# A GRU in front of a transformer block: the n gate's input products gather in bank 4, and ScalarE copies them over

## The chip, the cores and the metric

One core of one Trainium2 chip runs the whole program. The metric is the device time of one execution in microseconds. The kernel before takes 801.4 us, the median of 3 runs (801.28 to 802.28).

## The reference, cut to what matters

16 sequences of 128 time steps with 256 features each go through a GRU, and the result, added to its input, through one transformer block (layer norm with modulation, 16 heads of attention, an MLP). The change is in the GRU, which is a chain over 128 time steps:

```python
def cell(h, x):
    gi = x @ W_ih + b_ih            # 256 -> 768, needs only the input
    gh = h @ W_hh + b_hh            # 256 -> 768, needs the state
    i_r, i_z, i_n = split(gi, 3); h_r, h_z, h_n = split(gh, 3)
    r = sigmoid(i_r + h_r)
    z = sigmoid(i_z + h_z)
    n = tanh(i_n + r * h_n)
    return (1 - z) * n + z * h
```

The n gate is the one in which the input product and the state product can't be added before the gate r is known.

## The kernel before, in words

The 128 time steps are cut into 16 blocks (`r` in the code, `NBL`) of 8 steps (`s`, `BS`). The state lies turned: 128 partitions, and 32 columns `j` (two halves of the features, 16 sequences each). All products are made of float16 halves: `high*high`, `low*high` and `high*low`.

Each block has three PSUM banks, and they alternate between two sets, so that the next block's input products can be made while this block runs. The r bank and the z bank hold 8 x 32 columns each, and in them 16 columns of an output tile lie together. The n bank holds 8 x 32 pairs: in each pair, element 0 takes the state's product and element 1 the input's. VectorE's scan at L986 reads the pairs in order, with r beside them, and so forms `r*h_n + i_n` in one instruction. Because of the pairs, an input product of the n gate (`gate_cols`, `m` 4 or 5) writes every second column of its bank.

What one step does, and on which engine (a "step" below runs from one `h_hi` scan to the next):

- TensorE: `gru_step` issues 36 matmuls of 16 columns (24 at L439 with `h_hi`, 12 at L446 with `h_lo`), and waits for the state `h_hi` first. Behind them come the steps' other products: the transposes of a finished block at step 0 (L393) and at step 5, the bias of the next block's banks at step 1 (`x_bias`, L373), and from step 2 on the next block's input products (`x_products`, L386): 36 a block, of 128 columns each. `share` says how many: 9, 9, 7, 1, 5, 5 at the steps 2 to 7. The order `products` goes through the output tiles `m` = 0 to 5, so the n gate's 12 (tiles 4 and 5) come last: one at step 4, one at step 5, five at each of the steps 6 and 7.
- ScalarE: the sigmoid of r (L761), of z and of minus z (L763, L764), the tanh (L766), and then one piece of work beside the chain: the high half of the next x, of a stretch of weights, or of a finished block's rows (L731, a 128x256 copy out of PSUM). At step 3 there is none.
- VectorE: the scan `npre` (L986, behind a wait at L984), `nu` (L992), the scan `h_hi` (L998), the same in float32 (L1000), `h_lo` (L1003), and then work beside the chain.

The order on each engine is written out by hand, and semaphores tie the engines. In the last block TensorE has no input products; at its steps 1 to 4 it makes the modulation's products (`modulation`, L414) in bank 4. The attention and the MLP follow, on the same banks.

Of the kernel before, what the change touches and what calls it, by code (L numbers as in the profile page):

```python
# [15 lines left out]
P = 128  # L16
B, T, D = 16, 128, 256
KD = D // P
GATES = 3 * D
GM = GATES // P  # L20
# [8 lines left out]
BS = 8  # L29
NBL = T // BS  # L30
GB = KD * B
# [7 lines left out]
GK = 32 + 2 * GM  # L39
# [22 lines left out]
def build(nc, x, cols_in, gate_rows, W_ih, W_hh, ada_a, ada_r, ada_b, weights, out):  # L62
# [3 lines left out]
    with ctx:  # L66
# [29 lines left out]
        gpair = sb("gpair", [GK, P], f16, gru)  # L96
        sel = sb("sel", [GK, 2 * GM], f32, gru)
        selrz = sb("selrz", [GK, 4], f32, gru)
        pick = sb("pick", [GK, 4 * GB], f16, gru)
# [79 lines left out]
        def sems(names):  # L179
            return [sem(n) for n in names.split()]  # L180
# [11 lines left out]
        (r_mm, hn_mm, z_mm, r_ok, z_ok, n_ok, npre_ok, u_ok, hhi_ok, h32_ok, hlo_ok) = sems(  # L192
            "r_mm hn_mm z_mm r_ok z_ok n_ok npre_ok u_ok hhi_ok h32_ok hlo_ok")

        xt_hi, xt_lo = sems("xt_hi xt_lo")

        xr_ok, lb_T, lb_st, lb_ag, lb_ve, lb_r, lb_a, lb_b, lb_B, lb_hi, lb_lo = sems(
            "xr_ok lb_T lb_st lb_ag lb_ve lb_r lb_a lb_b lb_B lb_hi lb_lo")
# [15 lines left out]
        r_cols, z_cols = ([ps[:, 0:BS * GB].rearrange("p (t j) -> p t j", t=BS) for ps in pair]  # L214
                          for pair in (r_bank, z_bank))
        n_cols = [ps[:, :].rearrange("p (t j s) -> p t j s", t=BS, s=2) for ps in n_bank]
        row_ps, back_ps = bank[5][:, 0:D], bank[5][:, D:2 * D].rearrange("p (k c) -> p k c", k=KD)

        xr_v = xr[:, :, :, :].rearrange("p k n (b t) -> p k b n t", b=B)
# [142 lines left out]
        def _(pe):  # L362
            def product(ps, w, a, start, stop):
# [3 lines left out]
                mm(ps, w[1], a[0], start=False, stop=False, skip_group_check=True)  # L367
                return mm(ps, w[0], a[1], start=False, stop=stop, skip_group_check=True)  # L368

            def x_bias(n):  # L370

                for ps, at, width in ((r_bank, 0, GB), (z_bank, GB, GB), (n_bank, 2 * GB, 2 * GB)):
                    nc.tensor.matmul(ps[n % 2][:, 0:BS * width], gpair[:, :],  # L373
                                     pick[:, at:at + width].unsqueeze(1).broadcast_to([GK, BS, width]), start=True,
                                     stop=False, skip_group_check=True)

            def gate_cols(n, m):

                c = slice(m % 2 * B, (m % 2 + 1) * B)
                return (r_cols[n % 2][:, :, c], z_cols[n % 2][:, :, c], n_cols[n % 2][:, :, c, 1])[m // 2]  # L380

            def x_products(n, order):

                for m, k, i in order:
                    w, a = ((wih_hi, xb_hi), (wih_lo, xb_hi), (wih_hi, xb_lo))[i]
                    nc.tensor.matmul(gate_cols(n, m), w[:, k, m * P:(m + 1) * P], a[:, n % 2, k, :], start=False,  # L386
                                     stop=False, skip_group_check=True)

            def rows_T(n):

# [19 lines left out]
            def modulation(tiles):  # L410

                for m in tiles:
                    for k in range(KD):
                        mm = nc.tensor.matmul(bank[4][:, m * B:(m + 1) * B], adar[:, k, (m - G1) * P:(m - G1 + 1) * P],  # L414
                                              condT[:, k, :], start=(k == 0), stop=(k == KD - 1))
                if tiles[-1] == ADA - 1:
                    mm.then_inc(ada_mm, 1)
# [44 lines left out]
                high(2, slice(2, 8))  # L462
                low(2).then_inc(z_mm, 1)

            products = [(m, k, i) for m in range(GM) for k in range(KD) for i in range(3)]
            share = (0, 0, 0, 9, 18, 25, 26, 31, 36)
            for r in range(NBL):
                for s in range(BS):
                    gru_step(r, s)
                    if s == 0 and r > 0:  # L470
                        if r == 1:
                            pe.wait_ge(rows_ok, 2)
                        rows_T(r - 1)
                    elif s == 5 and r > 0:
                        rows_back(r - 1)
                    if r < NBL - 1:
                        if s == 1:
                            x_bias(r + 1)
                        elif s == 2:
                            pe.wait_ge(xt_lo, r + 2)  # L480
                        x_products(r + 1, products[share[s]:share[s + 1]])
                    if r == 0 and s == 3:
                        pe.wait_ge(adaw_in, 32)
                        pe.wait_ge(small_in, 16)
                        row_modulation(0)
                    elif r == 0 and s == 5:
                        row_modulation(1)
                    elif r == NBL - 1 and s in (1, 2, 3, 4):
                        if s == 1:
                            pe.wait_ge(rest_in, 16)  # L490
                        modulation(range(2 * s + 2, 2 * s + 4))
            rows_T(NBL - 1)

# [225 lines left out]
        def _(act):  # L719
# [5 lines left out]
            def x_high(n):  # L725
                act.wait_ge(x_in[n % 4], (n // 4 + 1) * 16)
                nc.scalar.activation(xb_hi[:, n % 2, :, :], x32[:, n % 4, :, :], copy).then_inc(xt_hi, 1)

            def y_high(n):
                act.wait_ge(lb_B, n + 1)  # L730
                nc.scalar.activation(y_hi[:, :, :, n * BS:(n + 1) * BS],  # L731
                                     back_ps.rearrange("p k (b t) -> p k b t", b=B), copy).then_inc(lb_hi, 1)
# [24 lines left out]
            for r in range(NBL):  # L757
                for s in range(BS):
                    t1 = r * BS + (s + 1)
                    act.wait_ge(r_mm, t1)  # L760
                    nc.scalar.activation(zr[:, :, 1], r_cols[r % 2][:, s, :], ACT.Sigmoid).then_inc(r_ok, 1)  # L761
                    act.wait_ge(z_mm, t1)
                    nc.scalar.activation(zg[:, :], z_cols[r % 2][:, s, :], ACT.Sigmoid).then_inc(z_ok, 1)  # L763
                    nc.scalar.activation(zz[:, :, 1], z_cols[r % 2][:, s, :], ACT.Sigmoid, scale=-1.0)  # L764
                    act.wait_ge(npre_ok, t1)
                    nc.scalar.activation(nu[:, :, 0], npre[:, :, 1], ACT.Tanh).then_inc(n_ok, 1)  # L766
                    if r == 0 and s == 0:
                        x_high(1)
                    if s == 1 and r < NBL - 2:
                        x_high(r + 2)  # L770
                    elif s in (2, 4, 6, 7):
                        piece_high(r * PB + (2, 4, 6, 7).index(s))
                    elif s == 5 and r > 0:
                        y_high(r - 1)
# [110 lines left out]
        def _(dve):  # L885
# [94 lines left out]
            for r in range(NBL):  # L980
                for s in range(BS):
                    t1 = r * BS + (s + 1)
                    dve.wait_ge(r_ok, t1)
                    dve.wait_ge(hn_mm, t1)  # L984

                    nc.vector.tensor_tensor_scan(npre[:, :, :].rearrange("p j s -> p (j s)"),  # L986
                                                 zr[:, :, :].rearrange("p j s -> p (j s)"),
                                                 n_bank[r % 2][:, s * 2 * GB:(s + 1) * 2 * GB], 0.0,
                                                 ALU.mult, ALU.add).then_inc(npre_ok, 1)
                    dve.wait_ge(z_ok, t1)  # L990
                    before = hs[:, 1 - r % 2, BS - 1, :, 1] if s == 0 else hs[:, r % 2, s - 1, :, 1]
                    tt(nu[:, :, 1], zg[:, :], before, ALU.mult).then_inc(u_ok, 1)  # L992
                    dve.wait_ge(u_ok, t1)
                    dve.wait_ge(n_ok, t1)

                    gates = (zz[:, :, :].rearrange("p j s -> p (j s)"), nu[:, :, :].rearrange("p j s -> p (j s)"),
                             0.0, ALU.mult, ALU.add)
                    nc.vector.tensor_tensor_scan(h_hi[:, :, :].rearrange("p j s -> p (j s)"), *gates  # L998
                                                 ).then_inc(hhi_ok, 1)
                    nc.vector.tensor_tensor_scan(hs[:, r % 2, s, :, :].rearrange("p j s -> p (j s)"), *gates  # L1000
                                                 ).then_inc(h32_ok, 1)
                    dve.wait_ge(h32_ok, t1)
                    tt(h_lo[:, :], hs[:, r % 2, s, :, 1], h_hi[:, :, 1], ALU.subtract).then_inc(hlo_ok, 1)  # L1003
                    if r > 0 and s in row_work:
                        row_work[s](r - 1)
                    if r == 0 and s == 0:
                        x_low(1)
                    if s == 2 and r < NBL - 2:
                        x_low(r + 2)
                    elif s == 6:  # L1010
                        rows_sum(r, slice(0, 6))
                    elif s == 7:
                        rows_sum(r, slice(6, BS))
                    if r == 0 and s in (3, 5):
                        row_modulation(s // 4)
                    elif r == NBL - 1 and s == 5:
                        modulation_sums()
                    elif r == NBL - 1 and s == 7:
                        modulation_gates()
# [214 lines left out]
```

## Time and profile before

| | |
|---|---|
| median of 3 runs | 801.4 us |
| the profiled execution's own time | 801.32 us |
| its span | 799.4 us |
| TensorE busy | 753.2 us (94%) |
| VectorE busy | 580.4 us (73%) |
| ScalarE busy | 470.9 us (59%) |
| GpSimd busy | 101.2 us (13%) |
| granted TensorE clock over the span, as a share of 2.4 GHz | 0.899 |

The GRU takes the first 273 us of the span. "Busy" of TensorE counts matmuls from the start to the modelled end of each, and they overlap, so it says little about idle room; the starts of two matmuls in a row say more. In a row of the timeline the first number is the start and the second the duration, both in us from the span's start. In a row that groups instructions, "| busy, mean ns | idle before, who ended it" stands at the end.

### The profile page before, as it was taken

What the parts mean: (1) busy time and instruction counts of PE and PEld (TensorE: products, weight loads), DVE (VectorE), ACT (ScalarE), POOL (GpSimd) and SP (SyncE); (2) the same over time, 40 slices, a digit from 0 to 9 for tenths busy, and PEclk for the clock granted to TensorE, in tenths of its full rate; (3) what the DMA queues carried; (4) which work ended last, traced back from release to release, by engine and by line L of the source; (5) the groups of instructions that cost most, each with busy time, mean ns of one, the idle gap of its engine ahead of it and who ended that gap; (6) DMA issues with size and microseconds to landing.
All of it is one profiled execution on the core that took longest, in us unless ns stands there. A gap on an engine that the chain in (4) does not pass through costs nothing.

```text
span 799.4 us, 24458 instructions
## 1 busy us (share of the span) xinstructions
PE 753.2 (94%) x10068; PEld 532.7 (67%) x10068; DVE 580.4 (73%) x1548; ACT 470.9 (59%) x1564; POOL 101.2 (13%) x121
## 2 busy tenths in 40 slices
PE   6888989889888889999999999999999999999998
PEld 5777777777777656666666666666667666644445
DVE  5677777777777567777788887788877888853543
ACT  4344444444443266667777667777677776766454
POOL 0221222222222200000030010020010300100130
PEclk9977665766877599999999999999999999999999
DMA  6121121112111012222222222222222222210001
GB/s 221 43 96 42 43 81 43 43 42 78 45 35 37 2 27 41 40 42 41 41 41 40 41 41 41 41 41 41 41 41 41 41 41 41 41 27 26 1 27 53
DMA packets 76566, 36.65 MB, mean 46 GB/s; under 512 B 70395, under 2 KB 73127, under 8 KB 76327
## 3 DMA queue, kind: packets, MB, share of 16 engines
q1 hardware_dynamic: 75879, 33.52, 18.3%
q8 instruction: 79, 1.29, 0.7%
q10 hardware_dynamic: 576, 1.57, 0.6%
q14 instruction: 32, 0.26, 0.1%
HBM read 16.20 MB, written 2.10 MB: 23 GB/s over the span
## 4 chain that ended last, share of the span: by engine, by line
PE 83%; ACT 6%; DVE 5%; DMA 2%; issue 2%; SPq 1%; DVEq 0%; ACTq 0%
PE bank L366 19%; PE bank L367 19%; PE bank L368 19%; PE bank L439 12%; PE bank L386 7%; PE bank L446 5%; DVE h_hi L998 3%; DMA pT_lo<-p_lo 2%; ACT zg L763 2%; ACT prob L812 1%; ACT nu L766 1%; PE bank L373 1%; PE bank L414 1%; ACT zz L764 1%; SPq L257 1%
## 5 line engine op out<-in xcount | busy, mean ns | idle before, releaser
L439 PE MATMUL bank<-h_hi,whh_hi 128*128 128x16 f16 x1536 | 112.8, 177 | 29.0 <-DVE h_hi L998 28.5
L439 PEld LDWEIGHTS bank<-h_hi,whh_hi 128*128 128x128 f16 x1536 | 92.7, 101 | 65.6 <-DVE h_hi L998 65.6
L366 PE MATMUL bank<-y_hi,w_hi 128*128 128x512 f16 (+2 forms) x324 | 122.6, 379 | 1.3 <-ACT hf L845 1.3
L367 PE MATMUL bank<-y_hi,w_lo 128*128 128x512 f16 (+2 forms) x324 | 122.6, 379 | 0.0
L368 PE MATMUL bank<-y_lo,w_hi 128*128 128x512 f16 (+2 forms) x324 | 122.3, 379 | 0.0
L439 PE MATMUL bank<-h_hi,whh_lo 128*128 128x16 f16 x1536 | 110.6, 176 | 0.0
L761 ACT ACTIVATE zr<-bank 128x32 f32<-128x32 f32 x128 | 25.7, 201 | 130.1 <-PE bank L446 130.1
L812 ACT ACTIVATE prob<-bank,nmx 128x128 f32<-128x128 f32 x256 | 90.4, 365 | 19.9 <-DVE nmx L1074 19.9
L439 PEld LDWEIGHTS bank<-h_hi,whh_lo 128*128 128x128 f16 x1536 | 93.4, 101 | 0.1
L366 PE MATMUL bank<-w_hi,y_hi 128*128 128x128 f16 x512 | 89.1, 219 | 0.0
L367 PE MATMUL bank<-w_hi,y_lo 128*128 128x128 f16 x512 | 89.1, 219 | 0.0
L368 PE MATMUL bank<-w_lo,y_hi 128*128 128x128 f16 x512 | 89.0, 219 | 0.0
L820 ACT ACTIVATE qT_hi<-bank,small 128x512 f16<-128x512 f32 x64 | 44.0, 687 | 74.0 <-PE bank L368 74.0
L446 PE MATMUL bank<-h_lo,whh_hi 128*128 128x16 f16 x1536 | 78.6, 176 | 0.0
L296 POOL TENSOR_TENSOR w_lo<-stage,w_hi 128x320 f16<-128x320 f32 x64 | 50.7, 792 | 193.7 <-DVE h_lo L1003 191.5
L986 DVE TENSOR_TENSOR_SCAN npre<-zr,bank 128x64 f32<-128x64 f32 x128 | 36.8, 287 | 47.4 <-ACT zr L761 47.3
L1071 DVE TENSOR_REDUCE mx<-bank 128x4 f32<-128x512 f32 x64 | 44.2, 690 | 29.4 <-PE bank L368 29.4
L386 PE MATMUL bank<-xb_hi,wih_hi 128*128 128x128 f16 x192 | 61.7, 326 | 3.2 <-DVE xb_lo L917 3.2
L386 PE MATMUL bank<-xb_lo,wih_hi 128*128 128x128 f16 x192 | 63.5, 334 | 0.0
L386 PE MATMUL bank<-xb_hi,wih_lo 128*128 128x128 f16 x192 | 62.1, 326 | 0.0
L446 PEld LDWEIGHTS bank<-h_lo,whh_hi 128*128 128x128 f16 x1536 | 59.1, 101 | 0.1
L368 PEld LDWEIGHTS bank<-y_lo,w_hi 128*128 128x128 f16 x324 | 31.8, 98 | 38.3 <-issue 1.0
(142 smaller groups left out, 2092.4 us busy)
## 6 DMA issues: line engine op xcount, KB each, us to landing
stage<-in_weights SPq DMA_DIRECT2D x16, 640.0 KB, 4.1
x<-in_x SPq DMA_DIRECT2D x16, 128.0 KB, 4.3
out<-yT SPq DMA_DIRECT2D x3, 512.0 KB, 2.6
adar<-in_ada_r SPq DMA_DIRECT2D x1, 1024.0 KB, 7.2
pT_hi<-p_hi SPq DMA_TRANSPOSE x64, 2.4
pT_lo<-p_lo SPq DMA_TRANSPOSE x64, 2.4
wih<-in_W_ih ACTq DMA_DIRECT2D x2, 384.0 KB, 4.0
whh<-in_W_hh ACTq DMA_DIRECT2D x2, 384.0 KB, 6.1
```

The lines of the kernel that those rows point to most:

```text
L296: gtt(w_lo[:, j * PC:(j + 1) * PC], stage[:, r % 2, i * PC:(i + 1) * PC], w_hi[:, j * PC:(j + 1) * PC], sub).then_inc(piece_lo, 1)
L366: mm(ps, w[0], a[0], start=start, stop=False, skip_group_check=True)
L367: mm(ps, w[1], a[0], start=False, stop=False, skip_group_check=True)
L368: return mm(ps, w[0], a[1], start=False, stop=stop, skip_group_check=True)
L386: nc.tensor.matmul(gate_cols(n, m), w[:, k, m * P:(m + 1) * P], a[:, n % 2, k, :], start=False, stop=False, skip_group_check=True)
L439: nc.tensor.matmul(out(m0 + m), half[:, k, w], h_hi[:, k * B:(k + 1) * B, 1], start=False, stop=False, skip_group_check=True)
L446: mm = nc.tensor.matmul(out(m0 + m), whh_hi[:, k, (m0 + m) * P:(m0 + m + 1) * P], h_lo[:, k * B:(k + 1) * B], start=False, stop=k == KD - ...
L761: nc.scalar.activation(zr[:, :, 1], r_cols[r % 2][:, s, :], ACT.Sigmoid).then_inc(r_ok, 1)
L812: op = nc.scalar.activation(prob[:, j, :], bank[3][:, j * T:(j + 1) * T], ACT.Exp, bias=nmx[:, j:j + 1], scale=SCALE, accum_out=den[:, j:j ...
L820: nc.scalar.activation(qT_hi[:, :], bank[0][:, :], ident_f, bias=bT[:, BQ + d % H:BQ + d % H + 1]).then_inc(q_h, 1)
L986: nc.vector.tensor_tensor_scan(npre[:, :, :].rearrange("p j s -> p (j s)"), zr[:, :, :].rearrange("p j s -> p (j s)"), n_bank[r % 2][:, s ...
L1071: nc.vector.reduce_max(mx[:, :], bank[3][:, :].rearrange("p (j s) -> p j s", j=QUAD), AX.X).then_inc(s_mx, 1)
```

## The change

The 12 input products of the n gate are made first of a block's 36, and into columns 256 to 511 of bank 4 (`xs_ps`), which nobody else uses in this part, laid out like the r bank: 16 columns of a tile together. Before the first of them a new matmul puts the n gate's input bias there (`side_bias`, 256 columns; its moving operand takes every second column of `pick`). When the last is done, ScalarE copies the 128x256 values into the elements 1 of the next block's n bank (`side_copy`, at step 3). `x_bias` is as before in what it issues. New semaphores: `xs_mm` (products done, ScalarE waits for it) and `xs_ok` (copied; VectorE waits for it before the first scan of a block, TensorE before the next block's `side_bias` and, in the last block, before each of the four modulation calls). Block 0's own products, made before the loop, stay as they were.

```diff
+        xs_ps = bank[4][:, BS * GB:2 * BS * GB].rearrange("p (t j) -> p t j", t=BS)
...
+            def side_bias(n):
+
+                if n > 1:
+                    pe.wait_ge(xs_ok, n - 1)
+                pick_x = pick[:, 2 * GB:4 * GB].rearrange("p (j s) -> p j s", s=2)[:, :, 1]
+                nc.tensor.matmul(xs_ps, gpair[:, :], pick_x.unsqueeze(1).broadcast_to([GK, BS, GB]), start=True,
+                                 stop=False, skip_group_check=True)
             def gate_cols(n, m):
                 c = slice(m % 2 * B, (m % 2 + 1) * B)
+                if m >= 4 and n > 0:
+                    return xs_ps[:, :, c]
                 return (r_cols[n % 2][:, :, c], z_cols[n % 2][:, :, c], n_cols[n % 2][:, :, c, 1])[m // 2]
             def x_products(n, order):
...
+                    if n > 0 and (m, k, i) == (GM - 1, KD - 1, 2):
+                        mm.then_inc(xs_mm, 1)
-            products = [(m, k, i) for m in range(GM) for k in range(KD) for i in range(3)]
+            products = [(m, k, i) for m in (4, 5, 0, 1, 2, 3) for k in range(KD) for i in range(3)]
...
                         elif s == 2:
                             pe.wait_ge(xt_lo, r + 2)
+                            side_bias(r + 1)
...
                     elif r == NBL - 1 and s in (1, 2, 3, 4):
+                        pe.wait_ge(xs_ok, r)
                         modulation(range(2 * s + 2, 2 * s + 4))
...
+            def side_copy(n):
+                act.wait_ge(xs_mm, n)
+                nc.scalar.activation(n_cols[n % 2][:, :, :, 1], xs_ps, copy).then_inc(xs_ok, 1)
...
+                    elif s == 3 and r < NBL - 1:
+                        side_copy(r + 1)
...
                     dve.wait_ge(r_ok, t1)
                     dve.wait_ge(hn_mm, t1)
+                    if s == 0 and r > 0:
+                        dve.wait_ge(xs_ok, r)
```

## Rows read from the trace of the kernel before

**Rows 1.** The page: the chain that ended last, by line; ScalarE's sigmoid of r.
```profile
PE bank L366 19%; PE bank L367 19%; PE bank L368 19%; PE bank L439 12%; PE bank L386 7%; PE bank L446 5%; DVE h_hi L998 3%; DMA pT_lo<-p_lo 2%; ACT zg L763 2%; ACT prob L812 1%; ACT nu L766 1%; PE bank L373 1%; PE bank L414 1%; ACT zz L764 1%; SPq L257 1%
...
L761 ACT ACTIVATE zr<-bank 128x32 f32<-128x32 f32 x128 | 25.7, 201 | 130.1 <-PE bank L446 130.1
```

**Rows 2.** Stretches: start:end, length, busy of each engine, granted clock, DMA.
```profile
12.11:255.28 243.17, 216.07 (x4972) 179.01 (x4970) 175.46 (x729) 105.12 (x569) 55.20 (x72) 0.71 0.18 54
...
273.35:278.60 5.25, 4.64 (x14) 2.18 (x15) 2.90 (x12) 0.38 (x1) 0.70 (x2) 0.50 0.02 5
```

**Rows 3.** Timeline of VectorE in block 15: the scans that end its steps.
```profile
256.98 0.29 DVE L998 TENSOR_TENSOR_SCAN h_hi<-zz,nu 128x64 f16<-128x64 f32 x1
258.96 0.29 DVE L998 TENSOR_TENSOR_SCAN h_hi<-zz,nu 128x64 f16<-128x64 f32 x1
261.00 0.29 DVE L998 TENSOR_TENSOR_SCAN h_hi<-zz,nu 128x64 f16<-128x64 f32 x1
263.67 0.29 DVE L998 TENSOR_TENSOR_SCAN h_hi<-zz,nu 128x64 f16<-128x64 f32 x1
...
271.03 0.29 DVE L998 TENSOR_TENSOR_SCAN h_hi<-zz,nu 128x64 f16<-128x64 f32 x1
273.06 0.29 DVE L998 TENSOR_TENSOR_SCAN h_hi<-zz,nu 128x64 f16<-128x64 f32 x1
```

**Rows 4.** Timeline where step 2 of block 8 ends, at the low clock.
```profile
148.47 0.29 DVE L998 TENSOR_TENSOR_SCAN h_hi<-zz,nu 128x64 f16<-128x64 f32 x1
148.47 0.31 PE L386 MATMUL bank<-xb_hi,wih_lo 128*128 128x128 f16 x1
...
148.58 0.31 PE L386 MATMUL bank<-xb_lo,wih_hi 128*128 128x128 f16 x1
...
148.82 0.19 PE L439 MATMUL bank<-h_hi,whh_hi 128*128 128x16 f16 x1
```

**Rows 5.** Timeline: n gate products (low clock, 7.7); r and z products (high clock, 13.2).
```profile
142.29 0.50 PE L386 MATMUL bank<-xb_hi,wih_lo 128*128 128x128 f16 x1
142.51 0.50 PE L386 MATMUL bank<-xb_lo,wih_hi 128*128 128x128 f16 x1
...
228.02 0.22 PE L386 MATMUL bank<-xb_lo,wih_hi 128*128 128x128 f16 x1
228.07 0.22 PE L386 MATMUL bank<-xb_hi,wih_hi 128*128 128x128 f16 x1
```

**Rows 6.** By line: duration in ns (min/median/max); moving operand stepped, then packed.
```profile
L439 PE MATMUL bank<-h_hi,whh_hi x1536: 168/174/302, 12.3 to 272.2; 128*128 128x16 f16 x192
...
L446 PE MATMUL bank<-h_lo,whh_hi x1536: 168/174/189, 12.9 to 272.3; 128*128 128x16 f16 x192
```

**Rows 7.** Stretches of steps 6-7, 0-1, 2-3, 4-5; first and last of 14.
```profile
41.34:45.30 3.96, 3.24 (x82) 2.69 (x82) 3.04 (x13) 1.99 (x10) 0.79 (x1) 1.00 0.00 0
...
251.26:255.28 4.02, 3.96 (x82) 3.41 (x82) 3.05 (x14) 1.95 (x10) 0.79 (x1) 0.60 0.01 4
...
29.37:33.34 3.97, 2.93 (x77) 2.27 (x77) 2.79 (x13) 1.58 (x9) 0.79 (x1) 1.00 0.00 0
...
239.07:243.19 4.12, 3.41 (x77) 2.43 (x77) 2.90 (x13) 1.25 (x8) 0.79 (x1) 0.84 0.03 6
...
33.34:37.37 4.03, 3.95 (x90) 3.59 (x90) 2.87 (x14) 1.59 (x9) 1.47 (x2) 0.58 0.43 104
...
243.19:247.25 4.06, 4.06 (x91) 3.68 (x90) 2.54 (x14) 1.59 (x9) 1.34 (x2) 0.50 0.40 102
...
37.37:41.34 3.97, 2.96 (x82) 2.46 (x82) 3.10 (x14) 1.90 (x10) 0.80 (x1) 1.00 0.26 100
...
247.25:251.26 4.01, 3.26 (x84) 2.69 (x82) 3.08 (x14) 1.88 (x10) 0.79 (x1) 0.82 0.17 67
```

**Rows 8.** By line: VectorE's stand-alone wait; ScalarE's copy out of PSUM.
```profile
L984 DVEq EVENT_SEMAPHORE  x128: 21/21/21, 13.3 to 272.3; - x128
...
L731 ACT ACTIVATE y_hi<-bank x15: 364/366/384, 40.9 to 269.0; 128x256 f16<-128x256 f32 x15
```

More of the change, by code:

```diff
@@ L193, in build @@
             "r_mm hn_mm z_mm r_ok z_ok n_ok npre_ok u_ok hhi_ok h32_ok hlo_ok")
-        xt_hi, xt_lo = sems("xt_hi xt_lo")
+        xt_hi, xt_lo, xs_mm, xs_ok = sems("xt_hi xt_lo xs_mm xs_ok")
         xr_ok, lb_T, lb_st, lb_ag, lb_ve, lb_r, lb_a, lb_b, lb_B, lb_hi, lb_lo = sems(
@@ L368, in product, with bias_rows @@
                 return mm(ps, w[0], a[1], start=False, stop=stop, skip_group_check=True)
+            def bias_rows(ps, at, width):
+                nc.tensor.matmul(ps, gpair[:, :], pick[:, at:at + width].unsqueeze(1).broadcast_to([GK, BS, width]),
+                                 start=True, stop=False, skip_group_check=True)
             def x_bias(n):
[L372 to L375, printed above, removed]
+                bias_rows(r_bank[n % 2][:, 0:BS * GB], 0, GB)
+                bias_rows(z_bank[n % 2][:, 0:BS * GB], GB, GB)
+                bias_rows(n_bank[n % 2][:, :], 2 * GB, 2 * GB)
+            def side_bias(n):
[4 more added lines that the diff above has]
+                                 stop=False, skip_group_check=True)
             def gate_cols(n, m):
                 c = slice(m % 2 * B, (m % 2 + 1) * B)
+                if m >= 4 and n > 0:
+                    return xs_ps[:, :, c]
                 return (r_cols[n % 2][:, :, c], z_cols[n % 2][:, :, c], n_cols[n % 2][:, :, c, 1])[m // 2]
@@ L385, in x_products @@
                     w, a = ((wih_hi, xb_hi), (wih_lo, xb_hi), (wih_hi, xb_lo))[i]
-                    nc.tensor.matmul(gate_cols(n, m), w[:, k, m * P:(m + 1) * P], a[:, n % 2, k, :], start=False,
-                                     stop=False, skip_group_check=True)
+                    mm = nc.tensor.matmul(gate_cols(n, m), w[:, k, m * P:(m + 1) * P], a[:, n % 2, k, :], start=False,
+                                          stop=False, skip_group_check=True)
+                    if n > 0 and (m, k, i) == (GM - 1, KD - 1, 2):
+                        mm.then_inc(xs_mm, 1)
             def rows_T(n):
```

## The prediction

> **What bounds the kernel now.** I read the page's chain of waits first. Besides the attention's and the MLP's matmuls it holds the GRU's lines: TensorE at L439 and L446, VectorE's scan at L998, ScalarE at L763 and L766, and TensorE at L386 with 7% [rows 1]. The last is the line that the change speeds up, so the question is whether these products are really on the way. For that I went to the timeline, one step at a time. The change lies wholly in the GRU.
>
> A step is a ring: the state `h_hi`, 36 small matmuls, the sigmoid of r, the scan `npre`, the tanh, the scan `h_hi`. The reader should see in [rows 3] that it takes one of two times. From 256.98 to 258.96 it is 1.98 us, from 271.03 to 273.06 it is 2.03 us. The granted clock makes the difference: 1.98 at 2.4 GHz, 2.03 at 1.2 GHz. Over blocks 0 to 14 the granted clock is 0.71 on average, so about 42% of the 120 steps run at the high level ((0.71 - 0.5) / 0.5) [rows 2].
>
> The input products fill the time in which TensorE waits for the ring. At the end of step 2 of block 8, at the low clock, the last product starts at 148.58. Products of this kind follow each other every 107 ns there (148.47, 148.58, rounded), so TensorE is done taking columns at 148.69. The new state is there at 148.76 (148.47 + 0.29), and the next step's first matmul starts at 148.82 [rows 4]. TensorE has 0.13 us to spare. This is the fullest kind of step. Steps with five slow n gate products hold nothing up either: steps 6 and 7 of block 14 last 4.02 us together, which is one step of 1.98 and one of 2.03 [rows 7]. So the products of L386 are in the chain of waits only as TensorE's previous instruction, not as what sets the step's length. **A faster n gate product is worth nothing by itself.**
>
> **The change part by part.** All sums are against the profiled execution's own time, 801.32 us, which is 0.1 us under the median of 801.4; I use the median as the base.
>
> *The n gate's products become faster.* An n gate product takes 0.22 us to the next at the low clock (142.29 to 142.51, with 0.50 us of duration); an r or z product takes 0.107 [rows 4], and 0.05 at the high clock (228.02 to 228.07) [rows 5]. In the new place 16 columns lie together as in the r bank, so I take the r bank's spacing. Per block 12 x 0.107 = 1.3 us of TensorE's time goes at the low clock, 12 x 0.053 = 0.6 us at the high one. All of it lies beside the ring, in steps 4 to 7: directly 0 us. Bounds: it can't lose, since nothing waits longer, and can't gain, since those steps are already 1.98 or 2.03 long like the bare steps of block 15 [rows 3].
>
> *The new bias matmul.* It has 256 columns and stands in step 2, the fullest one: twice an r product's spacing, 0.21 us, at the low clock. The spare room is 0.13 us, so the next step's 36 matmuls start 0.08 us late, and they head the ring, so all of it passes on. Nearly every step 2 is at the low clock: the stretches of steps 2 and 3 have 0.58 and 0.50 in the first and the last of 14, and 0.53 on average [rows 7]. 15 x 0.08 = **+1.2 us**. At the high clock the nine products take half the time and it would be hidden. Ends: 0, if the clock is high; 15 x (0.08 + 0.21) = +4.4, if the stepped read of `pick` halves its speed. A stepped read of float16 stands in the trace: `h_hi` is read at every second column and `h_lo` packed, and both take 174 ns in the median, where at half the speed 16 columns at 1.2 GHz would cost 13 ns more [rows 6]. So I take the full speed.
>
> The Trainium skill says the same in "SBUF — State Buffer", section "Door 1: The DMA port swizzle": TensorE's operands can step without loss as long as two reads fall into one 16-byte line. And on the other side PSUM's lines are 8 bytes, which it says slows matmuls with any gaps; the 0.22 against 0.107 agrees. By that rule too the bias costs 1.2 and not 4.4.
>
> *ScalarE's copy.* 128x256 out of PSUM took 366 ns at L731 [rows 8]; here it also writes into PSUM with gaps, which no row shows: between 0.37 us and twice that. It comes after the tanh in step 3, where ScalarE has no other work. Its products are done by then: the third product of step 3. ScalarE is idle 130.1 us before 128 sigmoids of r, 1.02 us each [rows 1], and that time, of a step without side work even more, covers both ends. Behind it in the queue is only the next sigmoid. Cost 0; twice the copy would still fit.
>
> *The new waits.* TensorE's (before `side_bias`) and ScalarE's are met long before. VectorE's at step 0 is met too (the copy is at step 3 of the block before), but it makes one more stand-alone wait just before the scan `npre`, which is in the ring. Such a wait is 21 ns [rows 8]; a hand-over by semaphore is 60 ns (148.76 to 148.82) [rows 4]. I take 0.03 x 15 = **+0.45 us**, with ends 0 and 0.9. Four TensorE waits in block 15: under 0.05 together.
>
> *What the change does to the clock.* This is the part that the page hides. In the blocks 1 to 14 I took the granted clock of the stretches of two steps, and averaged the 14: 0.70 in steps 6-7, 0.79 in steps 0-1, 0.53 in steps 2-3, 0.78 in steps 4-5 [rows 7]. The two high stretches each come behind one in which TensorE never rests at the low clock: 3.96 us busy of 4.02 in steps 6-7 and 4.06 of 4.06 in steps 2-3. The two in which it falls come behind stretches with 2.93 of 3.97 and 2.96 of 3.97. So the clock follows TensorE's work with a delay, and steps 6-7 owe their work to the slow writing of ten n gate products, 0.21 us each. With 0.107 they lose half of it and look like the steps 4-5 do now. Then the rise in steps 0-1 goes, and part of the level in steps 6-7. The high share in steps 0-1 is (0.79 - 0.5) / 0.5 = 0.6 of 30 steps, 18; I let 15 of them go, and of 12 in steps 6-7 let 9 go, while steps 2-5 stay as they are. 24 steps x 0.045 us (between 1.98 and 2.03) = **+1.1 us**. Ends: all of the 50 high steps go, +2.3; all 70 low ones become high, -3.2.
>
> *Block 15.* Its modulation products fill TensorE at the low clock. Steps there take 2.67 us (261.00 to 263.67) where a bare one takes 2.03; step 1, whose products ran at the high clock, cost nothing extra (258.96 to 261.00 is 2.04) [rows 3]. That high clock came from the n gate products of block 14's steps 6-7. Without it this step too costs 0.64: **+0.65 us**, with ends 0.65 and -1.9 (three slow steps become free).
>
> Sum: 1.2 + 0.45 + 1.1 + 0.65 = **+3.4 us**, so 801.4 + 3.4 = **804.8 us**. The stretch at the low clock behind the GRU (5.25 us [rows 2]) can come out up to 1 us longer or shorter, as the end of the GRU meets the rise of the clock.
>
> The Trainium skill ("TensorE: Matmul & The Clock Gate", section "What's actually happening") says that the clock is low by default, that work releases it and that idleness takes it back. That the work must stay away for it to fall would be another result: TensorE has no long idle stretch in either kernel, so the clock part would be 0. The trace speaks against that, as it falls behind stretches that are 74% busy.
>
> **The rivals.**
>
> *The clock stays as it is.* For it: why the clock falls is read from 14 stretches of one execution, and total work changes by little over a tenth. Against it: the positions in the block are so regular. Then 1.2 + 0.45 = +1.65: **803.0**.
>
> *The bias matmul reads at half the speed.* Against it are [rows 6], where the expected 13 ns would show. 3.4 + 3.2 = +6.6: **808.0**.
>
> *Faster: the clock comes out higher.* The place is steps 2 to 5: products plus one more bias lie closer together there, and if the release then holds on, the fullest steps run at 2.4 GHz. The bias is hidden there (0), 70 low steps give 3.2 us back, block 15 up to 1.9, less 0.45: -4.65, **796.8**. It decides from where over two thirds of the GRU's steps are at the high level. Against it: the work per block falls, and the stretches of steps 2-3 are busy all the time already.
>
> *It does not do what it says*, and writing to bank 4 is as slow as to the n bank. Then nine products in step 2 take 0.96 us more at the low clock, and the three in step 3 0.3: 15 x 1.2 = +18, **about 820**. Against it: the layout is that of the r bank.
>
> **How the numbers follow.** A change within 0.2% (1.6 us, so 799.8 to 803.0) can't be told from none. The forecast has 0.62, the clock as before 0.22, the slow read 0.07, the faster case 0.05, slow writing 0.02, something else 0.02. Slower by over 0.2%: nearly all of the forecast (0.57), half of the unchanged clock (0.10) and the two slow cases: 0.76. Within: 0.19. Faster: 0.05. The forecast's own range is 803.3 to 806.3 (waits 0 to 0.9, clock 0.5 to 1.8, the stretch behind the GRU 1 either way). The range 802.3 to 806.8 takes in the unchanged clock and leaves out the slow read and the far ends.
>
> **What would show it.** The spacing of the first nine products of step 2 is 0.107 at the low clock (right) or 0.21. The first GRU matmul of step 3 starts 0.14 us and not 0.06 after the scan's end; if 0.06, the bias term is wrong. The granted clock of blocks 0 to 14 is about 0.61 and that of steps 0-1 near 0.55; if it is 0.7, the clock term is. Step 1 of block 15 takes 2.67. The scan `npre` at step 0 comes 20 to 60 ns later than in other steps. The copy ends before the next sigmoid of r. The prediction as a whole fails if the clock rises, or if a copy or a wait holds the ring where I see room.

## The result, and the profile after

The changed kernel takes 805.96 us (median of 5, 805.79 to 807.74), the kernel before 801.4 (median of 5). The ratio is 1.0059, with an interval of 1.0044 to 1.0073: it is slower, by 4.6 us. Run again later beside other kernels it took 807.46 against 800.27, ratio 1.0089 (1.0074 to 1.0103), so the two kernels lie between 4.6 and 7.2 us apart. The forecast of 804.8 had the sign, and its range held the first value but not the second. Two of its terms had the right size, the bias matmul's was a quarter of what it is, the waits' does not show, and block 0 came out longer without a term for it.

The profiled execution took 807.74 us (span 805.8), the longest of the five. It is 6.4 us above the profiled one of before. The spans of the other four are 803.9 to 804.4. What follows takes this pair of traces apart, so it explains 6.4 us, and not the 4.6 between the medians.

Stretches of the kernel after: start:end, length, busy of the engines, granted clock. They are blocks 0 to 14, block 15, and the low stretch behind the GRU.
```profile
12.11:262.50 250.39, 219.09 (x4987) 180.97 (x4985) 175.40 (x729) 109.06 (x584) 55.14 (x72) 0.60 0.16 53
262.50:281.28 18.78, 16.21 (x324) 15.24 (x324) 11.65 (x50) 6.73 (x37) 3.72 (x5) 0.50 0.01 3
281.28:285.80 4.52, 3.91 (x12) 1.91 (x13) 2.48 (x11) 0.34 (x1) 0.55 (x1) 0.50 0.01 2
```
Blocks 0 to 14 are 7.2 us longer (250.39 for 243.17) at a clock of 0.60 for 0.71 [rows 2]. With block 15 the GRU ends at 281.28 instead of 273.35, 7.9 us later, and 1.5 of them come back before the end of the span; of these the low stretch behind the GRU, 4.52 for 5.25 us, is a part.

Where the fullest step ends, timeline of the kernel after, block 8, the stretch that answers to [rows 4]:
```profile
151.86 0.17 PE L456 MATMUL bank<-h_hi,whh_lo 128*128 128x16 f16 x1
...
152.08 0.39 PE L387 MATMUL bank<-pick,gpair 44*128 44x256 f16 x1
152.40 0.29 PE L401 MATMUL bank<-xb_hi,wih_hi 128*128 128x128 f16 x1
152.48 0.31 PE L401 MATMUL bank<-xb_hi,wih_lo 128*128 128x128 f16 x1
152.59 0.31 PE L401 MATMUL bank<-xb_lo,wih_hi 128*128 128x128 f16 x1
...
152.69 0.29 DVE L1026 TENSOR_TENSOR_SCAN h_hi<-zz,nu 128x64 f16<-128x64 f32 x1
...
153.23 0.31 PE L401 MATMUL bank<-xb_lo,wih_hi 128*128 128x128 f16 x1
153.33 0.22 PE L456 MATMUL bank<-h_hi,whh_hi 128*128 128x16 f16 x1
153.41 0.18 PE L456 MATMUL bank<-h_hi,whh_lo 128*128 128x16 f16 x1
```
The n gate's products are 0.107 us apart, as in the r bank. But `side_bias` (L387) has 0.32 us to the first product, where 256 columns would take 0.21 at the r bank's spacing. The state is there at 152.98, and the next step's first matmul starts at 153.33, 0.35 us later instead of 0.06. The next scan shows the step's length, 2.35 us (from 152.69 to 155.04):
```profile
152.69 0.29 DVE L1026 TENSOR_TENSOR_SCAN h_hi<-zz,nu 128x64 f16<-128x64 f32 x1
154.39 0.29 DVE L1014 TENSOR_TENSOR_SCAN npre<-zr,bank 128x64 f32<-128x64 f32 x1 [0.66 <-ACT zr L785]
155.04 0.29 DVE L1026 TENSOR_TENSOR_SCAN h_hi<-zz,nu 128x64 f16<-128x64 f32 x1
```

Steps 0-1, 2-3, 4-5 and 6-7 of block 1 in the kernel after, as [rows 7] have them for before:
```profile
30.86:34.92 4.06, 3.62 (x77) 2.56 (x77) 2.78 (x14) 1.53 (x9) 0.79 (x1) 0.50 0.00 0
...
34.92:39.30 4.38, 4.38 (x92) 3.94 (x91) 2.87 (x15) 1.88 (x10) 1.48 (x2) 0.50 0.46 140
...
39.30:43.31 4.01, 2.96 (x84) 2.51 (x82) 3.08 (x14) 1.90 (x10) 0.79 (x1) 0.91 0.15 51
...
43.31:47.37 4.06, 3.35 (x82) 2.82 (x82) 3.05 (x14) 1.94 (x10) 0.79 (x1) 0.51 0.00 0
```
Averaged over blocks 1 to 14 the granted clock is 0.50 in steps 0-1, 0.50 in steps 2-3, 0.77 in steps 4-5 and 0.56 in steps 6-7. Before it was 0.79, 0.53, 0.78 and 0.70. Only the rise behind steps 2-3 is left, and in block 1 TensorE now is busy 3.35 of 4.06 us in steps 6-7.

Block 15's scans, VectorE of the kernel after, as in [rows 3]:
```profile
264.24 0.29 DVE L1026 TENSOR_TENSOR_SCAN h_hi<-zz,nu 128x64 f16<-128x64 f32 x1
266.26 0.29 DVE L1026 TENSOR_TENSOR_SCAN h_hi<-zz,nu 128x64 f16<-128x64 f32 x1
268.93 0.29 DVE L1026 TENSOR_TENSOR_SCAN h_hi<-zz,nu 128x64 f16<-128x64 f32 x1
271.60 0.29 DVE L1026 TENSOR_TENSOR_SCAN h_hi<-zz,nu 128x64 f16<-128x64 f32 x1
274.26 0.29 DVE L1026 TENSOR_TENSOR_SCAN h_hi<-zz,nu 128x64 f16<-128x64 f32 x1
276.93 0.29 DVE L1026 TENSOR_TENSOR_SCAN h_hi<-zz,nu 128x64 f16<-128x64 f32 x1
```
Four steps take 2.67 us; before there were three.

By line in the kernel after: the copy, in ns.
```profile
L751 ACT ACTIVATE bank<-bank x15: 368/368/368, 20.3 to 254.0; 128x256 f32<-128x256 f32 x15
```
It takes 368 ns, as good as the copy to SBUF with its 366 [rows 8]. VectorE's further wait at step 0 shows nothing: `npre` starts 1.08 us after the end of the scan before it, in block 8's step 0 (147.98) as in its step 1 (150.01, against the scan at 148.63 + 0.29). Averaged over blocks 1 to 14 it is 1.09 us in both steps.

### The profile page after: what moved, and what is told of

It is laid out like the page before. It is cut to its first block, busy times and chain, and to the rows that moved or that the text cites. A ratio compares the mean times of both kernels' runs of the same rounds, so it can differ in the third digit from the quotient of the medians.

```text
span 805.8 us, 24518 instructions
## 1 busy us (share of the span) xinstructions
PE 756.1 (94%) x10083; PEld 535.4 (66%) x10083; DVE 580.2 (72%) x1548; ACT 474.7 (59%) x1579; POOL 101.1 (13%) x121
## 4 chain that ended last, share of the span: by engine, by line
PE 86%; ACT 5%; DVE 4%; DMA 2%; issue 2%; SPq 1%; DVEq 0%; ACTq 0%
PE bank L367 20%; PE bank L369 20%; PE bank L368 20%; PE bank L456 12%; PE bank L463 5%; PE bank L401 4%; DVE h_hi L1026 3%; ACT zg L787 2%; PE bank L373 2%; DMA pT_lo<-p_lo 1%; ACT nu L790 1%; PE bank L431 1%; ACT zz L788 1%; PE bank L387 1%; DVE nu L1020 1%
## 5 line engine op out<-in xcount | busy, mean ns | idle before, releaser
L456 PE MATMUL bank<-h_hi,whh_hi 128*128 128x16 f16 x1536 | 114.7, 179 | 33.0 <-DVE h_hi L1026 32.3
L456 PEld LDWEIGHTS bank<-h_hi,whh_hi 128*128 128x128 f16 x1536 | 96.1, 104 | 66.5 <-DVE h_hi L1026 66.4
L456 PEld LDWEIGHTS bank<-h_hi,whh_lo 128*128 128x128 f16 x1536 | 95.7, 104 | 0.3 <-issue 0.3
L401 PE MATMUL bank<-xb_hi,wih_hi 128*128 128x128 f16 x192 | 55.3, 293 | 2.3 <-DVE xb_lo L943 2.3
L401 PE MATMUL bank<-xb_lo,wih_hi 128*128 128x128 f16 x192 | 57.4, 302 | 0.0
L401 PE MATMUL bank<-xb_hi,wih_lo 128*128 128x128 f16 x192 | 57.0, 299 | 0.0
```

Of the source, the lines that this page charges most:

```text
L401: mm = nc.tensor.matmul(gate_cols(n, m), w[:, k, m * P:(m + 1) * P], a[:, n % 2, k, :], start=False, stop=False, skip_group_check=True)
L456: nc.tensor.matmul(out(m0 + m), half[:, k, w], h_hi[:, k * B:(k + 1) * B, 1], start=False, stop=False, skip_group_check=True)
```

## The experiments

The kernels of each group ran on one chip beside the same runs of the kernel before (800.91, 800.71 and 800.27 us). Ratios are to the kernel before.

**Is it the stepped read?** The kernel after with a packed operand:
```diff
-                pick_x = pick[:, 2 * GB:4 * GB].rearrange("p (j s) -> p j s", s=2)[:, :, 1]
+                pick_x = pick_in[:, :]          # 32 values in a row, made once by GpSimd
```


> The changed kernel, with the moving operand of side_bias packed (a tile of its own, 32 values in a row) instead of every second column of pick. In the changed kernel the first product starts 0.32 us after side_bias at the low clock, where its 256 columns take 0.21. Theory (the 44-row weights of the bias between 128-row weights cost the rest): nothing changes, step 3 lasts 2.35 us, ratio to the kernel before 1.0055 to 1.006. Rival (the stepped read of pick is slow): the product starts 0.21 us after the bias, step 3 lasts 2.24, 15 x 0.11 = 1.6 us less, ratio 1.004.

807.68 us, ratio 1.0085 (1.0066 to 1.0104). The product still starts 0.33 us after the bias (35.68, 36.01), and step 3 lasts 2.35. The read is not what costs. The ratio is higher than the first one of the changed kernel, and the same as its second.

**Is it the 44 rows?** The bias as a 128-row product, `gpair` and the copy of `pick` filled up with zeros:
```diff
-                nc.tensor.matmul(xs_ps, gpair[:, :], pick_x.unsqueeze(1).broadcast_to([GK, BS, GB]), ...
+                nc.tensor.matmul(xs_ps, gpair[:, :], pick_x.unsqueeze(1).broadcast_to([P, BS, GB]), ...
```


> The changed kernel, with side_bias as a 128-row product: gpair and a copy of the n gate's part of pick are filled up with rows of zeros, so the result is the same; the read of the copy is stepped as before. Theory (changing between weights of 44 and 128 rows costs about 0.19 us a time): side_bias starts 0.08 us earlier and the product behind it 0.21 us after it, step 3 lasts 2.11 to 2.16, 15 x 0.19 to 0.24 = 2.9 to 3.6 less than the changed kernel, 802.4 to 803.2. Rival (any bias or any first write to bank 4 costs it): as the changed kernel, 806.

804.23 us, ratio 1.0042 (1.0027 to 1.0057). TensorE's timeline of this kernel in block 3:
```profile
67.50 0.17 PE L461 MATMUL bank<-h_hi,whh_lo 128*128 128x16 f16 x1
...
67.63 0.37 PE L392 MATMUL bank<-pick_in,gpair 128*128 128x256 f16 x1
67.80 0.31 PE L406 MATMUL bank<-xb_hi,wih_hi 128*128 128x128 f16 x1
67.90 0.31 PE L406 MATMUL bank<-xb_hi,wih_lo 128*128 128x128 f16 x1
...
68.65 0.31 PE L406 MATMUL bank<-xb_lo,wih_hi 128*128 128x128 f16 x1
68.75 0.22 PE L461 MATMUL bank<-h_hi,whh_hi 128*128 128x16 f16 x1
```
The bias starts 1.04 us into its step, the 44-row one 1.12, and the first product 0.17 us behind it instead of 0.32. Together, 0.08 and 0.15, that is the 0.22 us by which step 3 shortens, from 2.35 to 2.13 (68.33 to 70.46 between the scans). What is left, 0.10, is about what 256 columns leave over in a step with 0.13 us of room, which the forecast had at 0.08. So shown: a 44-row matmul between 128-row ones costs about 0.22 us more than one of 128 rows. Whether the rows of the weights or those of the moving operand count isn't, as both were filled up, nor why: the rows of the trace show only when matmuls start. The time is 1 us above the range that I wrote, which started from the changed kernel's first result; its second is 3.2 above e7, and in the traces blocks 1 to 14 are 3.3 us shorter.

**Does the place matter?** `side_bias` at step 0, where there is room:
```diff
+                        if s == 0:
+                            side_bias(r + 1)
-                            side_bias(r + 1)        # at s == 2
```


> The changed kernel, with side_bias moved from step 2 to step 0, where TensorE has about 0.6 us to spare at the low clock. Theory (the cost is that the fullest step got a bias): steps 3 last 2.03 again, 15 x 0.32 = 4.8 us less than the changed kernel, so about 801.2 to 801.8; what is left over the kernel before, about +2 in the GRU, is the lower clock and block 15, part of it given back behind the GRU. Rival (ScalarE's copy, the waits or the bank are what costs): 805 or more.

804.29 us, ratio 1.0043 (1.0027 to 1.006). All scans around there are 2.02 to 2.04 apart again (148.11, 150.13, 152.17, 154.19), so step 3 is no longer than the others, and the GRU ends at 276.30 instead of 281.28, as expected. The total is 2.5 us above what I wrote. In the GRU there remain 2.95 us over the kernel before: 1.3 in block 0, 0.7 in block 15 and 0.9 in between, at a clock of 0.61. My mistake was to let part of it be given back behind the GRU; in this execution nothing came back, and what follows the GRU is 2.5 us longer than in the trace of before (528.5 for 526.0). Of the 1.3 in block 0, 1.1 can't be put down to the change (see block 0 below).

**Is slow writing real, and is it hidden by room alone?** The kernel before with the new order, still into the n bank:
```diff
-            products = [(m, k, i) for m in range(GM) for k in range(KD) for i in range(3)]
+            products = [(m, k, i) for m in (4, 5, 0, 1, 2, 3) for k in range(KD) for i in range(3)]
```


> The kernel before, with only the order of the products changed (n gate first), still written to the n bank with gaps. Theory (writing with gaps costs 0.21 us a product at the low clock, and only room in the step hides it): in step 2 nine of them take 1.92 us instead of 0.96 and the next step starts about 0.85 us late, in step 3 three of them cost another 0.2; 15 x 1.05 = +16, less what the fuller step lifts the clock: 812 to 818. Rival (the 0.21 us is an artefact of the order or of the end of the block): under 804.

814.66 us, ratio 1.0173 (1.0155 to 1.0191). In step 2 of block 8 the products are 0.21 us apart (154.75, 154.96, 155.17), and step 3 takes 2.86 (155.15 to 158.01). So the new place in bank 4 does what it is for: without it this order costs 13.7 us. In the old order the same slow products cost nothing.

**Is it the work that moves the clock?** e2 with ten matmuls a block that nobody needs, in steps 6 and 7:
```diff
+                        fill((0, 0, 0, 0, 0, 0, 5, 5)[s])   # 128x128, constant weights, unread columns of bank 4
```


> The kernel of e2 (bias in step 0) with five extra 128x128 matmuls in each of the steps 6 and 7, of constant weights with themselves, into columns of bank 4 that nobody reads. They give TensorE back there, as added work, the time that the slow n gate products took. Theory (the granted clock follows TensorE's work with a delay, and the faster products let it fall): the granted clock of blocks 0 to 14 rises from about 0.62 to about 0.70, steps 0 and 1 are mostly 1.98 us again, and the whole is 1 to 2 us shorter than e2, although it does more. Rival (the clock's level has to do with something else, or extra work only costs): as e2 or longer, about 804.3 or more.

799.6 us, ratio 0.9988 (0.9978 to 0.9999), 4.7 us less than e2 for 150 matmuls more. Blocks 0 to 14 of this kernel, and steps 0-1 of block 1:
```profile
12.11:256.61 244.50, 221.08 (x5140) 189.01 (x5137) 175.32 (x729) 109.67 (x584) 55.18 (x72) 0.69 0.18 54
...
30.35:34.32 3.97, 3.14 (x78) 2.36 (x78) 2.79 (x14) 1.58 (x9) 0.79 (x1) 1.00 0.00 0
```
The clock is back at 0.69, and at 0.81 in steps 0-1, on average over 14 blocks. In the GRU that gave 0.95 us, 0.6 of it in blocks 1 to 14. In the traces another 4.6 lie behind it (528.5 and 523.9 us from the GRU's end to the span's); both are of the slowest execution of their kernel. So the clock's answer to the work is shown, and that the larger part of the 4.7 comes from it is not: what it is stays open.

**How far does that go?** The kernel before, with such matmuls in all steps (525 in blocks 0 to 14, 32 in the last):
```diff
+                    if r < NBL - 1:
+                        fill(bank[4][:, 2 * P:3 * P], (7, 6, 1, 1, 4, 8, 4, 4)[s])
+                    else:
+                        fill(bank[2][:, 0:P], (8, 0, 0, 0, 0, 8, 8, 8)[s])
```


> The kernel before, with extra matmuls of the same kind in all steps of a block (7, 6, 1, 1, 4, 8, 4, 4 in the steps 0 to 7, and 8, 0, 0, 0, 0, 8, 8, 8 in the last block), 525 + 32 in all, read by nobody. Theory (work lifts the clock): the granted clock of blocks 0 to 14 goes from 0.71 to over 0.85, most steps take 1.98 us, the GRU ends 1 to 3 us earlier, and the attention starts at the high clock sooner: 1 to 5 us faster than the kernel before, 796 to 800. Rival (extra work is never free): slower than 801, by up to 525 x 0.1 us where it doesn't fit into the steps.

794.68 us, ratio 0.9924 (0.9909 to 0.9939), 6.0 us faster than the kernel before. Blocks 0 to 14, and steps 2-3 of block 1:
```profile
12.11:251.99 239.88, 217.83 (x5487) 192.63 (x5484) 175.52 (x729) 106.33 (x569) 55.19 (x72) 0.98 0.18 55
...
32.36:36.33 3.97, 3.33 (x95) 2.93 (x92) 2.88 (x14) 1.63 (x9) 1.47 (x2) 1.00 0.39 92
```
The clock is at 0.98, nearly every step takes 1.98 to 2.00 us, and the GRU ends at 270.28, 3.1 us earlier, of which 2.3 are in blocks 1 to 14. Behind the GRU this trace is another 3.8 us shorter (522.2 for 526.0), and no experiment here takes that part apart.

**Does the change itself cost anything at the high clock?** e2 with extra matmuls in all steps:
```diff
+                        if s == 4:
+                            pe.wait_ge(xs_ok, r + 1)
+                        fill(bank[4][:, 0:P], (5, 6, 1, 0, 5, 8, 8, 8)[s])
```

> The kernel of e2 with extra matmuls in all steps (5, 6, 1, 0, 5, 8, 8, 8, and 8, 0, 0, 0, 0, 8, 8, 8 in the last block). In steps 6 and 7 eight of them beside five fast products take about what five slow products and three take. Theory (at the high clock nothing of the change matters, since every step has room): as e5 within 1 us, 796 to 800. Rival (the change has a cost of its own beside bias and clock, as its copy or its waits): longer than e5 by over 1.5 us.

797.55 us, ratio 0.9958 (0.9942 to 0.9975). The GRU ends at 269.89, 0.4 us before e5's, but that hides two differences. Block 15 is 0.9 us shorter (17.35 for 18.29), as one of its slow steps fell away and another became shorter. Blocks 1 to 14 are 0.8 us longer (224.41 for 223.60), all of it in steps 5 to 7 at a granted clock of 0.95 or more. There this kernel has more extra matmuls than e5 (24 a block for 16), so the comparison can't tell a cost of the change from one of the extra work; in steps 0 to 4, where the bias and the copy are, the two are alike within 0.1 us in sum. The whole is 2.9 us above e5: behind the GRU 524.3 us against 522.3 in the two traces. So the total went the rival's way, and the GRU is within the theory's 1 us. What makes the attention longer, with the same code there, I could not settle.

**Block 15.** Its modulation products moved to step 0 of the blocks 7 to 14, alone (e10) and on top of e5 (e9, with 4 extra matmuls for 7 in those steps and 8 in every step of block 15):
```diff
-                    elif r == NBL - 1 and s in (1, 2, 3, 4):
+                    elif 7 <= r < NBL - 1 and s == 0:
...
-                        modulation(range(2 * s + 2, 2 * s + 4))
+                        modulation(range(G1 + r - 7, G1 + r - 6))
```


> The kernel before with the modulation moved like that and no extra matmuls. Theory: three slow steps of block 15 save 1.9 us; at the low clock one tile makes step 0 of a block late by up to 0.2 us, which happens in about 3 of 8 blocks: 1.3 us less, about 799.6. Rival (the clock falls by the work taken out of block 15, and the attention starts later at the high clock): 801.

798.82 us, ratio 0.9981 (0.9972 to 0.999). Block 15 takes 16.1 us instead of 18.1. Blocks 0 to 14 take 0.65 more, and that is all in block 0, to which nothing was done; blocks 1 to 14 are the same within 0.1 us (225.82 for 225.91).

> e5 with the modulation's products moved out of the last block: one tile at step 0 of each of the blocks 7 to 14, and the extra matmuls there cut from 7 to 4; in the last block 8 extra matmuls in every step. Theory (block 15's slow steps are its modulation at the low clock): all of block 15 takes 1.98 a step, e5's three steps of 2.65 to 2.67 and one of 2.32 go, 2.3 us less than e5, about 792.4, and the attention begins at the high clock. Rival (those steps wait for something else, or one tile at step 0 is too much): as e5, 794.5 or more.

793.02 us, ratio 0.9907 (0.9892 to 0.9922), the fastest version: 7.3 us under the kernel before and 14.4 under the changed one. Blocks 0 to 14 and block 15 of this kernel:
```profile
12.11:251.92 239.81, 219.46 (x5496) 194.91 (x5492) 175.76 (x729) 106.33 (x569) 55.22 (x72) 0.98 0.18 55
251.92:267.95 16.03, 14.26 (x356) 12.71 (x356) 11.67 (x50) 6.84 (x37) 3.72 (x5) 0.79 0.01 3
```
Eight steps in 16.03 us; e5 needed 18.29. The total is 0.6 us above what I wrote.

**The changed kernel again**, beside these two.

> The changed kernel itself once more, beside the two others of this call, to have it against the same runs of the kernel before: 805.5 to 807, ratio 1.0055 to 1.0075, steps 3 of 2.35 us, four steps of 2.67 in block 15.

807.46 us, ratio 1.0089, above the range that I gave from its first result. Its trace has the same steps: 2.35 us for step 3, 281 for the end of the GRU. The difference between the two measurements (4.6 and 7.2 us) is larger than their intervals, and no step of the GRU explains it. The two traced executions are alike, 807.74 and 807.46 us; it is the other four of the first measurement that are shorter, 805.8 to 806.4, and they left no trace.

## Why the prediction was right, by its own steps

*The faster products are worth nothing by themselves*: right. Their spacing fell from 0.21 to 0.107 as forecast, steps 4 to 7 kept their 1.98 or 2.03, and e3 shows that it is the room in the step that hid them.

*The bias matmul, +1.2*: the place and the mechanism were right, the size was not. It is 15 x 0.32 = 4.8. The failed step is "twice an r product's spacing": I priced 44-row weights by a 128-row product's row, and no row of a 44-row matmul between others stood in my sum, although step 1's bias (L373) is one. The trace of before shows the smaller part of the cost, the 0.08 us in front: behind the last `h_lo` group this bias starts after 0.19 us, an r product after 0.10. The 0.15 behind it stands in no row there, as the next matmul waits for the state.
```profile
48.22 0.25 PE L446 MATMUL bank<-h_lo,whh_hi 128*128 128x16 f16 x4
48.41 1.03 PE L373 MATMUL bank<-pick,gpair 44*128 44x256 f16 x3
...
50.25 0.25 PE L446 MATMUL bank<-h_lo,whh_hi 128*128 128x16 f16 x4
50.35 0.27 PE L386 MATMUL bank<-xb_hi,wih_hi 128*128 128x128 f16 x1
```
The higher end that I gave (4.4) came from a slow read, which e1 excludes. e7 splits the 0.32 into 0.22 for the rows and 0.10 for the columns.

*The copy, 0*: right, 368 ns. *The waits, +0.45*: nothing shows of them.

*The clock, +1.1 in blocks 1 to 14*: right in place and about in size. 0.79 fell to 0.50 in steps 0-1 and 0.70 to 0.56 in steps 6-7; the changed kernel's second trace has 0.50 and 0.55. Without step 3, the steps of blocks 1 to 14 are longer by 1.3 us in sum. That the work is the cause was argued from positions only; e4 and e5 show that work lifts it, each by adding matmuls and getting the clock back. The reading that only a long idle stretch takes the clock back does not fit the kernel after either: in steps 4-5 of block 1 TensorE is busy 2.96 of 4.01 us, and the clock goes from 0.91 there to 0.51 in steps 6-7. What the Trainium skill says in "TensorE: Matmul & The Clock Gate", section "What's actually happening", that work releases the clock, agrees with e4 and e5.

*Block 15, +0.65*: right, 0.7, four steps of 2.67 for three.

*Block 0* is 1.5 us longer (18.75 for 17.26), of which 0.3 is its own bias. The rest, nearly all of it in one step (3.71 us for 2.59), had no term. The row modulation's float32 products in step 3 ran at the low clock and took 2.02 us, 1.08 before, and the next step waited for them. But this does not come from the change, as far as the traces show. The rows are of before, of the changed kernel, of e10, whose block 0 is the one of before, and of e7, which has the change:
```profile
20.19 1.08 PE L406 MATMUL bank<-adaw,small 128*128 128x256 f32 x4
...
20.70 2.02 PE L423 MATMUL bank<-adaw,small 128*128 128x256 f32 x4
...
20.09 1.90 PE L406 MATMUL bank<-adaw,small 128*128 128x256 f32 x4
...
20.86 1.08 PE L428 MATMUL bank<-adaw,small 128*128 128x256 f32 x4
```
e10 has the long step too (3.57 us) and e7 has not (2.53). It goes with where the clock stood low in that execution.

Sum in the GRU: 4.4 (step 3 of 14 blocks) + 1.3 + 0.7 + 1.5 = 7.9, as between the traces; without block 0's long step, which the change is not shown to cause, it is 6.8. What follows the GRU gave 1.5 back in these two executions. That the number came out near is in part luck. The forecast was +3.4, and its bias term was 3.6 too small. The waits' 0.45, which do not show, and the 1.5 given back behind the GRU stood against that, and the first measurement is 1.8 us under the difference of the traces. By the second measurement, 7.2 us, it was too low. Its own range of 803.3 to 806.3 is narrower than its ends allow, too: added up they give 802.8 to 807.0.

## What to carry to other kernels

Ask first whether a slow instruction is on the ring or in its shadow: here slow writes cost nothing in half-full steps and 13.7 us in the fullest ones, and a fix that puts one small matmul into the fullest step loses what no faster product can bring back. Where a chain through several engines sets the time, taking work off TensorE can cost clock, and work that nobody needs can pay, as it did here: price the clock by position, and try filler before tuning. Before a longer stretch is put down to a change, look for it in a variant that left that stretch alone, as e10 did with block 0. Price a matmul from a row with its own count of rows between the same neighbours.

## What the runs showed that I had not expected

- A 44-row matmul between 128-row ones costs about 0.22 us more than the same columns with 128 rows, at 1.2 GHz (step 3 of 2.35 against 2.13 us).
- 557 needless 128x128 matmuls made the kernel 6.0 us faster (ratio 0.9924), and the clock of the GRU's blocks went from 0.71 to 0.98. In the traces 3.1 us of it are in the GRU; the rest lies behind it and is not explained.
- Behind the GRU the same code took between 521.7 and 528.5 us in the twelve traces, only part of which is the low clock at its start (3.6 to 6.5 us long, absent in e9 and e6).
